# A gated cross-attention and feed-forward attention kernel: v and the heads' results move to DRAM, and their two projections are spread over the turns before and after

## What is computed

```python
def _L0_xattn_ref(x, context, Wq, Wk, Wv, Wo, bo):   # 8 heads of 64, context has 384 channels
    q = (x @ Wq).reshape(B, Nq, HEADS, DIM_HEAD)
    k = (context @ Wk).reshape(B, context.shape[1], HEADS, DIM_HEAD)
    v = (context @ Wv).reshape(B, context.shape[1], HEADS, DIM_HEAD)
    sim = jnp.einsum('bihd,bjhd->bhij', q, k) * SCALE
    attn = jax.nn.softmax(sim, axis=-1)
    out = jnp.einsum('bhij,bjhd->bihd', attn, v)
    out = out.reshape(B, Nq, HEADS * DIM_HEAD)
    return out @ Wo + bo
...
# _L0_ffn_ref: 16 heads of 32, self-attention with normalized q, then
    h = h.transpose(0, 2, 1, 3).reshape(Bsz, Nn, C)
    gates = jax.nn.softmax(h @ Wr.T + br, axis=-1)       # 15 routed, the best 3 kept
...
    sw = jax.nn.softmax(h @ Ws.T + bs, axis=-1)          # 2 shared
...
    out = h * masked_gates.sum(axis=-1, keepdims=True)
    return out @ Wp.T + bp
...
x = x + jnp.tanh(g_xattn[0]) * _L0_xattn_ref(_layernorm(x, axis=-1), ctx_768, ...)
x = x + jnp.tanh(g_ffn[0]) * _L0_ffn_ref(_layernorm(x, axis=-1), ...)
```

## Time and profile before

| | before |
|---|---|
| median of 3 runs | 5062.16 us |
| the three runs | 5056.38, 5062.16, 5085.25 us |
| the profiled execution | 5047.21 us, its span 5045.4 us |
| mean granted PE clock | 0.964 of 2.4 GHz |
| PE busy | 4586.3 us (91%) |
| POOL busy | 3357.6 us (67%) |
| DVE, ACT busy | 2949.3 us (58%), 2596.8 us (51%) |
| DMA | 481.06 MB |

### The profile page before, as it was taken

The page is one execution under the profiler, slowest core; times in us unless marked ns, Lnnn a source line. Parts: engine busy times, 40 slices in busy tenths (PEclk is TensorE's granted clock), DMA queues, the critical chain, the costliest instruction groups (busy, mean ns, idle before and its releaser), DMA issues.

```text
span 5045.4 us, 66897 instructions
## 1 busy us (share of the span) xinstructions
PE 4586.3 (91%) x21568; PEld 2358.1 (47%) x21568; DVE 2949.3 (58%) x3955; ACT 2596.8 (51%) x4705; POOL 3357.6 (67%) x2667
## 2 busy tenths in 40 slices
PE   4999999999999999988988888988888988989988
PEld 3554555555555555453444444543543533534534
DVE  5464646464545464656656656656656666666562
ACT  3445444444444444546646546556456466466464
POOL 2656566666666565648768668678478578578597
PEclk8999999999999999999999899999899999999998
DMA  7344444353434343322332222313213222232320
GB/s 240 101 136 114 125 123 126 119 132 120 109 121 109 119 111 113 89 94 70 86 88 59 76 84 59 105 55 84 84 51 84 84 68 68 84 84 60 101 51 26
DMA packets 285207, 481.06 MB, mean 95 GB/s; under 512 B 32832, under 2 KB 165440, under 8 KB 275648
## 3 DMA queue, kind: packets, MB, share of 16 engines
q1 hardware_dynamic: 284864, 476.79, 34.5%
HBM read 223.14 MB, written 50.33 MB: 54 GB/s over the span
## 4 chain that ended last, share of the span: by engine, by line
PE 38%; issue 8%; ACT 5%; POOL 4%; DVE 4%; DMA 2%; SPq 0%; ACTq 0%; POOLq 0%; DVEq 0%
PE aux L877 13%; PE aux L978 9%; PE aux L963 8%; POOL added_f L856 4%; PE aux L945 3%; ACT probs L1168 2%; PE aux L990 2%; DVE nm L1327 1%; DMA xs<-x_after_xattn 1%; PE aux L999 1%; PE aux L921 1%; ACT more L1168 1%; DMA out<-xs 1%; DVE halves_f L1345 1%; DVE st L1263 1%
## 5 line engine op out<-in xcount | busy, mean ns | idle before, releaser
L856 POOL TENSOR_TENSOR added<-added,probs 128x512 f32<-128x512 f32 x1433 | 1802.5, 1291 | 921.6 <-PE aux L978 657.1
L1327 DVE TENSOR_REDUCE nm<-aux 128x2 f32<-128x1024 f32 x1536 | 1810.4, 1220 | 791.4 <-PE aux L945 789.5
L1168 ACT ACTIVATE probs<-aux 128x512 f32<-128x512 f32 x2151 | 1190.5, 600 | 904.8 <-PE aux L963 837.3
L963 PE MATMUL aux<-stack 128*128 128x512 f32 x4096 | 1426.0, 440 | 127.7 <-ACT probs L1168 78.7
L963 PEld LDWEIGHTS aux<-stack 128*128 128x128 f32 x4096 | 711.6, 192 | 973.7 <-issue 365.1
L978 PE MATMUL aux<-probs,vh 128*32 128x512 f32 (+1 forms) x4302 | 991.0, 632 | 66.2 <-ACT vh L1135 21.0
L856 POOL TENSOR_TENSOR added_f<-added_f,probs 128x512 f32<-128x512 f32 x537 | 677.4, 1295 | 184.0 <-PE aux L978 131.1
L945 PE MATMUL aux<-ck_hi,cq_hi 32*128 32x512 f32 (+1 forms) x3072 | 460.8, 492 | 158.2 <-DVE nm L1327 109.4
L877 PE MATMUL aux<-xT_hi,wqk 128*128 128x512 f32 x1536 | 583.2, 416 | 4.1 <-DVE xT_lo L1290 2.0
L945 PEld LDWEIGHTS aux<-ck_hi,cq_hi 32*128 32x128 f32 (+1 forms) x3072 | 182.9, 188 | 633.1 <-issue 618.2
L1168 ACT ACTIVATE more<-aux 128x512 f32<-128x512 f32 x537 | 302.3, 602 | 149.9 <-PE aux L963 111.0
(11 more groups left out here) (132 smaller groups left out, 4800.9 us busy)
## 6 DMA issues: line engine op xcount, KB each, us to landing
wqk<-w_split SPq DMA_DIRECT2D x256, 256.0 KB, 3.8
wvo<-w_split SPq DMA_DIRECT2D x64, 1024.0 KB, 6.9
stack<-cq_hi SPq DMA_DIRECT2D x128, 256.0 KB, 5.1
stack<-ck_hi SPq DMA_DIRECT2D x128, 256.0 KB, 5.0
stack<-cq_hi SPq DMA_DIRECT2D x256, 128.0 KB, 2.3
stack<-ck_hi SPq DMA_DIRECT2D x256, 128.0 KB, 2.4
xs<-in_x SPq DMA_DIRECT2D x16, 1024.0 KB, 6.7
stack<-cq_lo SPq DMA_DIRECT2D x64, 256.0 KB, 4.9
```

Source lines behind the costliest of these rows:

```text
L856: pool.tensor_tensor(onto, onto, exp_buffer(T, e), ALU.add).then_inc(added_ok, 1)
L963: ins = pe.matmul(out, stack[:, g % 2, e * ph.SLOTS + ks, jt * P:(jt + 1) * P], stack[:, g % 2, e * ph.SLOTS + qs, n * HALF:(n + 1) * HALF ...
L1168: act.activation(exp_buffer(T, e), aux[:, o.bank["S", T, e], :], ACT.Exp, scale=ph.SCALE).then_inc(probs_ok, 1)
L1327: dve.tensor_reduce(nm[:, half, first:first + 2 * TT - t:TT], aux[:, b:b + 2, :], axis=AX.X, op=ALU.max, negate=True).then_inc(emptied["dv ...
```

## The change

`vh` goes away. v is computed one turn ahead, tile by tile: in the due times of the new table at steps 38 to 59 of the turn before (X) or 39 to 60 (F), one tile each 3 steps. Each tile passes through `v_out` into the DRAM tensor `v_kept` (`vs`), and each group loads its 128 columns into one of two halves of `v` (`vl`). The result of a half of a group is multiplied straight out of PSUM into `h_raw` (no `cp`), split there into hi and lo, and both are stored in `h_kept` (`hw`). `op` runs one turn later, from `parts` with two slots that `ol` loads (due from step 1.5 with 1.69 between tiles in X, from -1.13 with 3.73 between in F). In F the gate logits are summed by group: 4 small matmuls for each half (`gt`) and an add in SBUF (`ga`). The context is loaded in three pieces through a smaller `raw`; `qwork` is smaller; POOL's additions are items of their own for each head; the assumed costs and the whole table `AT` are new, and `run` charges PE for changes of tiling. The number and the shapes of matmuls stay as they are.

```diff
+      dict(p=[0.69, 18.6, 36, 50], over=6.09, mx0=-5.5, mxn=12.04, load=[51.51, 62.62], norm=[43.61, 30.7], turned=[30.5, 37.03], vp=[39, 3], out=[-1.13, 3.73], xr=-13.34, off={"trl": -0.94, "ad": -2.39, "tra": 1.65, "l2": 2.38, "cp": -4.87, "hsl": 0.44, "ev": -0.54, "ln": -0.9, "hs": -1.11, "sma": -1.35, "pqa": 1.36, "pkl": 0.75, "s3": 0.52, "pka": -0.28, "ssa": -0.53}))
...
-            if T % TURN < TT:
-                after += [("vpe", TT * j + T % TURN)]
-            self.add(("PV", T), "pe", 1.05, T + 0.9, after)
+            after += [("vl", T // STEPS)]
...
-                self.add(("cp", h), "act", 0.6, T + 0.95, [("PV", T), ("cp", h - 1)])
-                self.add(("sm", h), "pe", 0.9 * (1 + ph.APART), b, [("ad", T - ph.APART), ("ex", T, G - 1), ("sm", h - 1)])
-                self.add(("sma", h), "act", 1.3, b + 0.3, [("sm", h), ("ev", h - 1)])
-                self.add(("ev", h), "dve", 2.2, b + 0.6, [("sma", h), ("cp", h), ("ev", h - 1)])
+                b = T + 1
+                self.add(("sm", h), "pe", 0.86 * (1 + ph.APART), b, [("ad", T - ph.APART, G - 1), ("ex", T, G - 1), ("sm", h - 1)])
+                self.add(("sma", h), "act", 1.2, b + 0.3, [("sm", h), ("ev", h - 1)])
+                self.add(("ev", h), "dve", 2.07, b + 0.6, [("sma", h), ("PV", T), ("ev", h - 1), ("hw", h - 1)])
+                if ph.ffn:
+                    self.add(("gt", h), "pe", 0.45, b + 1, [("ev", h), ("fb", 0)])
+                    self.add(("ga", h), "dve", 0.2, b + 1.2, [("gt", h), ("gm", 2 * (h // HALVES - 1) + h % 2)])
+                self.add(("hs", h), "act", 0.55, b + 1, [("ev", h)])
+                self.add(("hsl", h), "dve", 0.6, b + 1.2, [("hs", h), ("gt", h)])
...
+        ph, b0 = stage(j), TURN * (j - 1)
...
+            t, b = TT * j + i, b0 + ph.AT["vp"][0] + i * ph.AT["vp"][1]
+            source = [("trl", j, i // (TT // 2), NG - 1)] if ph.ffn else [("cxl", j, ph.KC - 1)]
             for k in range(whole):
-                self.add(("vp", TT * j + t, k), "pe", 0.69, b0 + t - 0.4 + 0.4 * k / whole, [("vp", TT * j + t, k - 1)] if k else [("wv", j)] + source + freed)
-            self.add(("vpe", TT * j + t), "dve" if ph.ffn else "act", 0.7, b0 + t, [("vp", TT * j + t, whole - 1)] + freed + ([("fb", 0)] if ph.ffn else []))
-        self.add(("wo", j), "sp", 1.3, b0 + TT, [("vp", TT * j + TT - 1, whole - 1), ("ws", ph.W + 3)])
+                self.add(("vp", t, k), "pe", 0.685, b + 0.4 * k / whole, [("vp", t, k - 1)] if k else [("wv", j), ("vp", t - 1, whole - 1)] + source)
...
+        for g in range(NG * j, NG * (j + 1)):
+            self.add(("vl", g), "sp", 0.65, (g - 1) * STEPS + 0.5, [("vs", TT * j + TT - 1), ("PV", (g - 1) * STEPS - 1), ("vl", g - 1)])
...
+        ph, at, b0 = stage(j), stage(j).AT, TURN * (j + 1)
+        whole = stage(j + 1).chunks("vp")
+        last = [("vp", TT * (j + 2) - 1, whole - 1)] if j + 1 < 2 * B else [("op", TT * j - 1, NG - 1)]
+        self.add(("wo", j), "sp", 1.3, b0 + at["out"][0] - 4, last + [("ws", ph.W + 3)])
...
-        vh = sb("vh", [P, HALVES + 1, HALF])
-        v = vh[:, 1:HALVES + 1, :].rearrange("p (g a) c -> p g (a c)", a=2)
...
+        h_raw = sb("h_raw", [P, HALF])
+        h_hi = sb("h_hi", [P, HALF], F32R)
+        v_out = sb("v_out", [P, DM])
+        v = sb("v", [P, 2, TT, P])
+        parts = sb("parts", [P, 2, 2, NG, P], F32R)
...
+        v_kept = nc.dram_tensor("v_kept", [2, NG, P, TT, P], F32).ap()
+        h_kept = nc.dram_tensor("h_kept", [2, TT, P, 2, NG, P], F32).ap()
...
+                    elif kind == "vs":
+                        j, t = divmod(g, TT)
+                        wait_emptied(sp, ("vp", g))
+                        if j >= 2 and t == 0:
+                            for i in range(2):
+                                sp.wait_ge(v_loaded[i], 16 * (NG // 2) * (j - 1))
+                        sp.dma_start(v_kept[j % 2, :, :, t, :].rearrange("g p c -> p g c"), v_out[:].rearrange("p (g c) -> p g c", g=NG)).then_inc(v_stored, 16)
+                    elif kind == "vl":
+                        j = g // NG
+                        sp.wait_ge(v_stored, 16 * TT * (j + 1))
+                        if g >= 2:
+                            sp.wait_ge(weighed, (g - 1) * STEPS)
+                        sp.dma_start(v[:, g % 2], v_kept[j % 2, g % NG]).then_inc(v_loaded[g % 2], 16)
+                    elif kind == "hw":
+                        j, h = divmod(g, HALVES)
+                        sp.wait_ge(h_lo_ok, g + 1)
+                        if j >= 2 and h < 2:
+                            for i in range(2):
+                                sp.wait_ge(h_loaded[i], 16 * (TT // 2) * (j - 1))
+                        for part, done in enumerate((h_hi[:].bitcast(F32), h_raw[:])):
+                            sp.dma_start(h_kept[j % 2, h % 2 * TT // 2:(h % 2 + 1) * TT // 2, :, part, h // 2, :].rearrange("t p c -> p t c"),
+                                         done.rearrange("p (t c) -> p t c", c=P)).then_inc(h_stored, 16)
+                    elif kind == "ol":
+                        j, t = divmod(g, TT)
+                        sp.wait_ge(h_stored, 32 * (HALVES * (j + 1) - 1 + t // (TT // 2)))
+                        if g >= 2:
+                            wait_full(sp, ("op", g - 2))
+                        sp.dma_start(parts[:, g % 2].bitcast(F32), h_kept[j % 2, t]).then_inc(h_loaded[g % 2], 16)
...
-                        if T % TURN < TT:
-                            wait_emptied(pe, ("vp", T // TURN * TT + jt))
+                        if T % STEPS == 0:
+                            pe.wait_ge(v_loaded[T // STEPS % 2], 16 * (T // STEPS // 2 + 1))
                         out = bank(it)
                         for e in range(G):
-                            ins = pe.matmul(out[e * D:(e + 1) * D, :], v[:, g, jt * P + e * D:jt * P + (e + 1) * D],
+                            ins = pe.matmul(out[e * D:(e + 1) * D, :], v[:, T // STEPS % 2, jt, e * D:(e + 1) * D],
                                             exp_buffer(T, e), start=jt == 0, stop=jt == TT - 1)
...
-                    elif kind == "cp":
-                        h = it[1]
-                        act.wait_ge(weighed, (h + 1) * TT)
-                        act.activation(vh[:, h % HALVES, :], aux[:, o.bank["acc", h], :], ACT.Copy).then_inc(copied, 1)
...
+                        wait_emptied(act, ("sm", h))
+                        act.activation(h_hi[:], h_raw[:], ACT.Copy).then_inc(h_hi_ok, 1)
...
+                        link(dve.scalar_tensor_tensor(rn[:], src, 2.0, rn[:], ALU.add, ALU.mult))
+                        dve.wait_ge(weighed, (h + 1) * TT)
+                        if h:
+                            dve.wait_ge(h_stored, 32 * h)
+                        dve.tensor_tensor(h_raw[:], aux[:, o.bank["acc", h], :], rn[:], ALU.mult).then_inc(emptied["dve"], 1)
```

342 lines of the change are left out of this document (154 added, 188 removed).

## The result

The changed kernel takes 5010.9 us (median of 6 runs, 4999.4 to 5017.8) beside 5059.3 us for the kernel before: a ratio of 0.989, 95% interval 0.986 to 0.993. It is faster by 1.1%, where 4.0% and 4858 us were forecast; the range ended at 5010. The profiled execution took 5007.0 us, 40.2 less than the one before.

The account below looks back on a forecast made before the run. PE alone was taken to bound X; in F, POOL paced the long attention stretch and PE's bunched projections the rest. Terms -246 + 32 + 6 + 5 = -203 gave 4844 us, and 15 for the median 4858; range 4720 to 5010.

Parts of the forecast that it names:

- The side list: Effects beside spreading the projections: bank +32 us, start +6, tail +5; cp, DRAM traffic, SP and op 0.
- p, the price of a projection matmul: Time each of 213 projection matmuls adds to an F turn beyond the scores' pace: 0.15 us chosen, bounds 0 and 0.233.
- a false 0.30: Price in us of each of 213 projection matmuls in the old F turn, from (373 - 309.3)/213.
- F turns of 330.9 us: Average F turn after spreading the projections, from 361.6 us: 30.7 less each, -246 us over eight.
- the long stretch: The 261 us of an F turn running attention, POOL 84% busy; its pace of 1.208 us a score gives 309.3 a turn.
- The bank, +32 us: Result's PSUM bank held 10.1 us longer in each of 64 F halves, costing 0.5 us a half.
- X, 0 with 20 us either way: Spreading gains nothing in X turns, since PE alone bounds them and has no idle time to fill.
- The start, +6 with a range to 20: First PV needs all eight tiles of v, coming at about 144 us instead of 106.4; most is caught up.
- DRAM and SP, 0: Four more DRAM transfers, some 201 MB in all, and 36 more DMAs a turn issued by SP cost nothing.
- The tail, +5: After the last ev, a store-and-load round trip of 7.7 us plus slots, less 4 for gate matmuls done earlier.
- What would show it: Signs for right: POOL's 31 us idle gone, F turns 325 to 337 us; for wrong: X turns over 260.
- nothing hides: Rival, chance 0.17: F's projection matmuls cost their full 0.233 us each, giving 4964 to 4996 us.

Follow-up runs that it names:

- gates_no_scalar: Changed kernel with DVE gate products written as reductions and the maximum given to ACT as exponential bias: 4892.3 us, ratio 0.962 to the kernel before.
- copy_back: Changed kernel with ACT's copy of the bank of results put back and the plan made anew: 5035.6 us, ratio 0.992 to the kernel before.
- The three attempts: Changed kernel with context due times moved, or readers of loads put later; short-gate-block kernel with X loads and start reordered: X turns 263.1, 263.0, 261.7 us.
- tiny_traffic: Changed kernel whose new transfers of v and results carry only a few bytes from the third turn on: 4967.9 us, ratio 0.979 to the kernel before.

## Why the prediction was right in direction and wrong in size

- **The side list lacked a term, and that is the step that failed.** The span fell by 40 us where 203 were forecast: 90 of the missing 163 are in F, 52 in X, 21 in the start. The list went through `cp`, the bank, DRAM, SP, `op`, the start and the tail, and said of DVE only where the bank is concerned. The gates summed by group meant tiles in SBUF, and so a block of 9.9 us on DVE for one of 3.6, twice a turn and beside POOL's adds. Taking that out brings 114 us in turns 8 to 15 (gates_no_scalar), more than all that F lacked. The diff showed it: operands named `aux` became `glog`, `gexp` and `gsum`.
- **p, the price of a projection matmul, was built on a false 0.30.** Leaving out a third of F's `op` and `vp` in the kernel before brings 0.13 us for each (0.07 to 0.18), where the prediction had 0.30; the rest of the 64 us a turn that it laid on 213 matmuls does not go with their number. In the changed order it is 0.05 to 0.08 by the ratios (0 to 0.15), with the gate block short nothing. The chosen 0.15 stands at the upper edge of the first of these and is too high for the second.
- **F turns of 330.9 us** would have been met but for the gate block: 329.6. That agreement is luck, and two misses stand in it. With p near 0 the step at the pace of the long stretch gives 300 us, which no version reached; something else of F's loop holds the other 30. DVE's queue is the part that answers most (8.4 us of operations more: 11 us a turn), POOL less (35 us fewer: 7.7), PE least (10 us fewer: 0 to 2 in the traces, 3 to 5 by the ratios). No run took work from ACT, though PE's largest wait in gates_no_scalar is for its exponentials, so what paces the rest stays open.
- **The bank, +32 us:** nothing of it is seen. Holding the bank costs no score (the rows of L1366); what freeing it early is worth by itself is not shown, since copy_back changed more than that.
- **X, 0 with 20 us either way:** +52 us. "PE has no idle time to fill" was right, and that made it overlook that PE has none to lose. The plan puts two loads of x, one of context and one of v into the blocks of copies to `stack`, and the change also took the second slot of `raw`, which the prediction did not mention. Of the 7.9 us a turn, 4.5 are PE waiting and 3.4 slower matmuls. Shown is that the waits followed here end with a transfer in that queue and that moving a reader moves the wait; not shown is which arrangement would avoid it. The three attempts brought back 0 to 1.2 us. A rival was not tried: DVE waits for POOL in X too. The step of the row maxima with both operands in SBUF (`nm<-nm`, four a turn) takes 0.83 us by the mean in X where it took 0.39. That part stays open.
- **The start, +6 with a range to 20:** +27. The working, seven intervals of 4.6 us, took a store's landing as 3.4 us; the DMA engines were at 0.97 to 0.99 there and ACT waited up to 13.5.
- **DRAM and SP, 0:** nearly right in F. The bytes of the new transfers from the third turn on cost 36 us of the whole (tiny_traffic; some 50 by the ratios), a few in each place.
- **The tail, +5:** +5.3. The prediction's estimate from the Trainium skill, +3, was further off; the section it draws on describes DMAs issued from GpSimd, and here SP issues them all.
- **A slip:** the sum as written, 5062.2 less 203, is 4859 and not 4858.
- **What would show it:** POOL's idle of 31 us at the change of F turns is gone (the longest between 3100 and 3800 us is 10.3 us) and F's clock is 0.96, PE 91% busy, all as said for "right"; X turns are over 260 us, as said for "wrong". No `PV` of F waits for a DMA. The total lies next to the rival "nothing hides" (4964 to 4996), but by another way: most of the matmuls' time hid, and DVE's operations did not.

## What to carry to other kernels

When a change moves a small tile from PSUM to SBUF, look at each DVE operation on it: with two operands in SBUF, or as a product with a number or a copy within SBUF, it can have to wait for POOL's operation, and its price is then that operation (1.3 us here), whatever its own size. Sums and products written as reductions over one tile, or a bias on ACT, avoid it; in the last turn a single such operation waited 35 us. And where several engines hand work on in a loop, price an edit by taking the work away or adding some, engine by engine; by busy shares (PE 91%, DVE 72%) PE would come first here, and F answered to DVE more.

## What was not expected of the hardware

- A DVE operation of the two-operand kind can wait through many operations of POOL, not one: 35.4 us at 4904, through some 28 of POOL's operations without a break.
- Not only operations with two tensors in SBUF wait for POOL: a product of 128x4 with a number took 0.8 us when it came first and 1.3 in 7 of 16 blocks further back, and a copy 1.3 in 7 of 16, where 0.16 suffices. A scalar operand in SBUF did not make `SCALAR_TENSOR_TENSOR` with a tensor in PSUM wait (0.22 us, 16 of 16).
- The clock can fall at a short wait of PE. At 1048.2 PE had been idle for 3.8 us; the six us from 1047 are granted 0.50, the 1.2 GHz level, and the twelve after it are at 0.99:

```profile
1047.00:1053.00 6.00, 4.80 (x12) 1.83 (x13) 3.07 (x3) 2.17 (x5) 5.84 (x4) 0.50 0.98 265
1053.00:1065.00 12.00, 12.00 (x51) 6.93 (x50) 9.19 (x26) 6.92 (x15) 10.68 (x9) 0.99 0.71 172
```

  In the kernel before, two idle pieces of 2.6 us went differently. After the one that ended at 908.7 the clock stayed at 1.00; after the one that ended at 3647.7 it fell (0.72 over these six us), so the length of the wait alone does not decide:

```profile
905.00:911.00 6.00, 3.40 (x14) 1.85 (x14) 4.28 (x20) 1.83 (x5) 6.00 (x6) 1.00 0.00 0
3646.00:3652.00 6.00, 4.29 (x14) 3.29 (x15) 3.92 (x4) 0.03 (x1) 0.00 (x0) 0.72 0.59 199
```
